# A macaron transformer block on one core: attention's eight half images begin at other slots, the last one has nine slots

## What is computed

```python
x = x + 0.5 * ffn(layernorm(x))
x = x + attention(layernorm(x))
x = x + 0.5 * ffn(layernorm(x))
```

## The kernel before

| list | half 0 to 7 |
|---|---|
| D_SLOT | 29, 37, 46, 55, 64, 72, 81, 90 |
| B_SLOT | 37, 46, 55, 64, 72, 81, 90, 98 |
| NORM_SLOT | 39, 48, 57, 66, 74, 83, 92, 100 |
| out | 41, 50, 59, 68, 76, 85, 94, 101 |
| EXP_SLOT | 31/33, 39/42, 48/51, 59/60, 66/69, 76/78, 83/86, 92/95 |

## Time and profile before

### The profile page before, as it was taken

One profiled execution on the slowest core, in us unless ns is written; L12 is line 12 of the kernel. 1 busy time (PEld: TensorE's weight loads), 2 busy tenths in 40 slices (PEclk: granted clock), 3 DMA queues, 4 the chain that ended last, 5 costly groups with the idle time before them and its releaser, 6 DMA issues.

```text
span 1469.7 us, 22015 instructions
## 1 busy us (share of the span) xinstructions
PE 1419.1 (97%) x7642; PEld 679.7 (46%) x7642; DVE 944.8 (64%) x1295; ACT 552.4 (38%) x1153; POOL 501.0 (34%) x424
## 2 busy tenths in 40 slices
PE   4999999999999999899999999999999999999998
PEld 2444444444444544445454444444444444444443
DVE  5778853333348989898889889979925733333243
ACT  4566323333233433345435454345233213333211
POOL 2321132221244475252625434444322122221353
PEclk9999999999999999999999999999999999999999
DMA  8999659887493467075526552445338168888594
GB/s 305 305 350 320 267 146 209 200 182 192 172 277 125 156 196 220 30 244 135 153 72 186 150 166 73 121 160 140 112 101 257 59 188 213 192 190 185 187 321 165
DMA packets 233724, 272.63 MB, mean 186 GB/s; under 512 B 132242, under 2 KB 156818, under 8 KB 230162
## 3 DMA queue, kind: packets, MB, share of 16 engines
q1 hardware_dynamic: 198594, 166.34, 39.7%
q10 hardware_dynamic: 23664, 67.66, 14.5%
q0 software_dynamic: 11360, 37.23, 9.4%
HBM read 168.39 MB, written 72.88 MB: 164 GB/s over the span
## 4 chain that ended last, share of the span: by engine, by line
PE 63%; DVE 10%; issue 8%; DMA 4%; POOL 2%; ACT 2%; SPq 1%; POOLq 0%; ACTq 0%; DVEq 0%
PE bank L1484 25%; PE bank L1607 13%; PE bank L1498 12%; PE bank L1632 7%; DVE region L1147 3%; DMA rows<-sorted_y,slots 1%; PE side L1120 1%; PE side L1620 1%; DVE region L1153 1%; POOL rows L665 1%; DMA x2d<-rows 1%; DVE sgh L1854 1%; PE side L1253 1%; DMA region<-region 1%; POOL hs L1812 1%
## 5 line engine op out<-in xcount | busy, mean ns | idle before, releaser
L1484 PE MATMUL bank<-xT,wb 128*128 128x512 bf16 x2688 | 615.5, 381 | 22.6 <-DMA xT<-region 17.6
L1484 PEld LDWEIGHTS bank<-xT,wb 128*128 128x128 bf16 x2688 | 257.7, 98 | 323.9 <-issue 29.2
L1812 POOL TENSOR_TENSOR hs<-sgh,hs 128x512 bf16<-128x512 f32 x126 | 161.9, 1285 | 629.1 <-ACT hs L1704 628.2
L1498 PE MATMUL bank<-wb,hs 128*128 128x512 bf16 x1536 | 358.0, 380 | 0.2 <-POOL hs L1812 0.2
L1498 PEld LDWEIGHTS bank<-wb,hs 128*128 128x128 bf16 x1536 | 147.8, 98 | 173.9 <-issue 2.9
L1607 PE MATMUL bank<-wr,region 128*128 x912 | 221.7, 379 | 0.0
L1704 ACT ACTIVATE hs<-sgh 128x512 bf16<-128x512 f32 x128 | 81.3, 635 | 340.2 <-DVE sgh L1854 337.4
L1854 DVE TENSOR_TENSOR sgh<-bank,sgh 128x512 f32<-128x512 f32 x128 | 87.9, 687 | 155.8 <-PE bank L1484 154.6
L1147 DVE TENSOR_TENSOR region<-region 128x1024 f32<-128x1024 f32 x128 | 183.0, 1454 | 0.9
L1801 POOL DMA_INDIRECT region<-xnd,idxs x78 | 74.6, 957 | 221.8 <-DMA region<-region 213.5
L1153 DVE TENSOR_REDUCE region<-region 128x256 f32<-128x2048 f32 x64 | 146.3, 2286 | 2.2
(11 more groups left out here) (182 smaller groups left out, 1351.6 us busy)
## 6 DMA issues: line engine op xcount, KB each, us to landing
wb<-wsplit ACTq DMA_DIRECT2D x42, 1024.0 KB
wb<-wsplit ACTq DMA_DIRECT2D x42, 512.0 KB, 4.4
sorted_y<-region SPq DMA_DIRECT2D x78, 256.0 KB
wsplit<-wb SPq DMA_DIRECT2D x8, 1536.0 KB, 7.4
wr<-wall SPq DMA_DIRECT2D x6, 1536.0 KB, 9.7
rows<-x SPq DMA_DIRECT2D x32, 256.0 KB, 4.9
region<-xln SPq DMA_DIRECT2D x128, 64.0 KB, 3.7
xnd<-rows SPq DMA_DIRECT2D x30, 256.0 KB, 4.0
```

The lines of the kernel that those rows point to most:

```text
L1484: m = e.matmul(ps[:], wb[:, w % 2, wp, at:at + P], xt[:, xp, c, :], start=(i == 0), stop=(i == 3 * NDC - 1))
L1498: m = e.matmul(psD[tt][:], hs[:, s % 2, hp, tt * P:(tt + 1) * P], wb[:, w % 2, wp, at:at + D], start=(first and i == 0), stop=(last and i ...
L1812: e.tensor_tensor(hs[:, s % 2, 1, :], sgh[:, s % 2, :], hs[:, s % 2, 0, :], ALU.subtract).then_inc(S("h_lo").sem, 1)
```

## The change

Three lists of slots get other values; no instruction is added or taken away.

```diff
-        EV_LOAD[0], EV_LOAD[1], EV_LOAD[2], EV_LOAD[3], EV_LOAD[5], EV_LOAD[6], EV_LOAD[8] = (
-            UNIT - 2, EV_AT[1] - 4, EV_AT[2] - 2, EV_AT[3] - 3, EV_AT[5] - 3, EV_AT[6] - 2, EV_AT[8] - 1)
+        EV_LOAD[0], EV_LOAD[1], EV_LOAD[2], EV_LOAD[3], EV_LOAD[4], EV_LOAD[5], EV_LOAD[6], EV_LOAD[8] = (
+            UNIT - 2, EV_AT[1] - 4, EV_AT[2] - 2, EV_AT[3] - 3, EV_AT[4] - 4, EV_AT[5] - 3, EV_AT[6] - 2, EV_AT[8] - 1)
...
-        D_SLOT = [ROUTED_AT[0] + 6 + 35 * h // 4 for h in range(HALVES)]
+        D_SLOT = [ROUTED_AT[0] + 6 + 9 * h - h // 3 for h in range(HALVES)]
         LOAD_SLOT = [ROUTED_AT[0] + 1, ROUTED_AT[0] + 5] + [d - 4 for d in D_SLOT[2:]]
-        B_SLOT = D_SLOT[1:] + [D_SLOT[-1] + 8]
+        B_SLOT = D_SLOT[1:] + [D_SLOT[-1] + 9]
```

## The result

The changed kernel took 1468.91 us in the median of ten runs (1466.22 to 1472.14), the kernel before, run between them, 1474.50 us (1469.81 to 1478.97). The ratio is 0.9964, 95% interval [0.9953, 0.9974]: 5.6 us or 0.36% faster, where 9.5 us were forecast. The forecast of 1463.4 us is missed by 5.5, of which 1.6 is the kernel before itself: its median is 1474.5 over ten runs, where the forecast started from 1472.9 over three. The result lies inside the range, a little above the point that was called faster. Of all runs behind this text one, of the kernel before, took 3854 us and is left out as slow.

What follows compares the result with a forecast made beforehand. TensorE's waits in attention were taken as all that a new order could give back. Terms 4.1 + 0.2 + 1.8 + 0 + 3.9 - 0.5 gave 9.5 us, from 1472.9 to 1463.4, range 1458.5 to 1470.5.

Steps and rivals of the forecast that it cites:

- half 1: Slots 40 to 47 with the combines: 6.4 us over the pieces falls to 2.3, seven combines falling in; gain 4.1.
- half 3: Slots 55 to 63: counted among nine-slot halves costing 0.1 us together; no gain or loss named.
- half 5: Slots 72 to 80, cut to eight slots: 2.0 us stays 2.0 (ends 0.5 and 5.4); gain 0.
- the routing: Slot 112 on: second routing list stands behind an evacuation, charged 0.5 us (0 to 1.5); later row gather stays hidden.
- half 7: Slots 90 to 98, given a ninth slot: 5.4 us over the pieces falls to 1.5; gain 3.9.
- half 4: Slots 64 to 71, given a ninth slot: silu and turn waits go, 2.1 us falls to 0.3; gain 1.8.
- half 2: Slots 48 to 54, cut to eight slots: slot 49's stall shrinks, 2.0 us falls to 1.8; gain 0.2.
- The drain of the table load: ScalarE's exp ahead of turn or out pieces: skill page's drain estimated at some 5.5 us against the change; left out.
- B: Rival, given back: eight slots cost wherever they are; gain 3 instead of 9.5 us, 1470.0; chance 0.15.
- D: Rival: VectorE's total is the same and waits only move to other slots; 1472.9 us; chance 0.05.
- A: Rival: halves 2 and 5 fit without stalls, half 1 leaves no residue; five us more, 1458.5; chance 0.14.
- C: Rival: VectorE overflows in halves 2 and 5 once over about 4.2 us behind TensorE; 1477.4 us; chance 0.06.

Runs made afterwards that it cites:

- run of three edits: Kernel before with nine slots in the last half, each half's first two qkv pieces later and the second eight combines one slot earlier: ratio 0.9974.
- the order alone: Kernel before with only the new order of halves 0 to 6, the last half keeping eight slots: ratio 0.9988.
- second comparison: The kernel before and the changed kernel run once more, both unchanged: ratio 0.9955 [0.9939, 0.9971].
- last half of nine alone: Kernel before with only the last half's ninth slot added, run twice: ratios 0.994 and 0.996.

## Why the prediction was half right

From the forecast gain of 9.5 us to the 4.2 between the two profiled executions: 2.4 too little in half 1, 2.0 lost in half 3, to which the sum gave no term, 2.1 lost in half 5, whose term was 0, and 0.2 in the routing; 1.1 more than forecast in half 7 and 0.3 more in half 4. The time lies inside the range by the range's width and by the clock, which no term of the sum names: at equal clock the gain is 3.4 us. As far as the sum goes that is luck.

**What bounds the kernel** was read rightly: TensorE's waits in attention are all that there was to gain, and the change moved only them.

**Half 7, 3.9 us forecast, 5.0 measured.** The mechanism and place are as said: the wait for L1198 in slot 99 is gone. The residue was put at 1.5 us and is 0.48, since t_out was in time and took ScalarE's two copies with it. The run with this edit alone shows the same 0.48.

**Half 1, 4.1 forecast, 1.7 measured (2.8 in the second execution).** This is the first step that failed. The wait for L1198 did shrink from 2.87 to 0.41, as forecast (that a moved combine does this shows in the run of three edits as well, where it went from 2.9 to 1.3), and with it went the clock's 1.7 us, which the sum had in its 4.3 without knowing it; slots 40 and 41 moved to 41 and 42 with 1.05 and 0.19 us, as forecast. What was not seen: half 2's rows are loaded from xln a slot later, too. SyncE's issues and the transposes that want them, in the kernel before and after:

```profile
554.95 3.86 SPq L1083 DMA_DIRECT2D region<-xln  x8
...
562.59 0.63 PE L1103 MATMUL side<-ident,region 128*128 128x128 f32 x4 [0.17 <-DMA region<-xln]
```

```profile
566.29 3.92 SPq L1083 DMA_DIRECT2D region<-xln  x8
```

The rows were there 7.6 us after the first issue before, and 8.7 after (574.95 above). In the seven executions that were looked at in which SyncE's order has this load a slot later, TensorE waited 0.8 to 2.5 us for it, and 0.2 at most in the six that have it and the combines where they were. In the slot to which it moved, ScalarE's queue issues a weight load of 1024 KB beside it (at 567.45), in the one that it left one of 512 KB (at 556.10), and the weights' queue took 38.7% of the DMA engines' time instead of 26.2%. That this is the reason is argued from these rows and was not tested by itself. The other wait that is new, of 1.1 us, for VectorE's L1854 in slot 44, is its backlog: a combine stands in that slot behind the 3.04 us wait for rows of x.

**Half 3, not costed, 2.0 lost.** The second failed step. The prediction counted half 3 in "nine slots each: 0.1 together" and asked only about length. But the half ahead of it lost a slot, so its tiles stand two slots ahead instead of three: slot 58 waits 0.72 for a third part, slot 62 1.12 for L1112. This was in the profile of before: half 5 there, nine slots behind one of eight, cost 2.0 for the same two waits. The prediction even names slot 61 as a place where exp comes to stand just ahead of a turn, but gives it no price. The term that it put at nothing is 2.0 us.

**Half 5, 0 forecast, -2.1 measured.** The third. Its ends were given as 0.5 and 5.4, and the value was left at 2.0 because "exp and turn stay neighbours". The overlap of VectorE's heavier slots with that turn is what it had wrong. Eight slots with the tiles three ahead is what half 7 was in the kernel before, and that cost 5.4. VectorE, 3.5 us late in slot 78 before, is 5.0 late now, and the wait for L1112 goes from 1.1 to 2.60. The experiment that gave it back its ninth slot took its 4.2 to 0.1.

**Half 4 (1.8 forecast, 2.1 measured) and half 2 (0.2 and 0.2)** hold. The silu wait only moved, from slot 49 (1.81) to slot 50 (1.62), where the text said that it would be under 1 us; and no wait for L1112 came up in slot 53, where one was forecast. The sum is right and its parts are not.

**The routing: 0.5 forecast, 0.7 measured.** The list is late by 0.60 us at 1188.52, and the first block of the second routing waits for nothing. The indices were done at 1191.2 instead of 1193, and the transposes were issued at 1195.09, forecast 1197. TensorE and VectorE there (it answers the earlier trace rows):

```profile
1188.52 0.75 PE L749 MATMUL side<-rows 128*128 128x78 bf16 x16 [0.60 <-DVE rows L743]
1189.11 1.46 PE L1498 MATMUL bank<-wb,hs 128*128 128x512 bf16 x6
...
1205.94 2.75 PE L1607 MATMUL side<-wr,region 128*128 x12
```

```profile
1191.21 0.20 DVE L758 TENSOR_TENSOR idxs<-rows 128x39 int32<-128x39 f32 x1
```

**The drain of the table load.** The Trainium skill, ScalarE: Activation LUTs, "What ACT_TABLE_LOAD costs", would have made exp in front of a turn cost some 1.4 us more for each load, by an estimate from its drain of about 1380 ns. The seven ScalarE rows above show two loads of 1.28 us with the ACTIVATE at once behind each (888.81 + 1.28 = 890.09, next at 890.11; 891.24 + 1.28 = 892.52, next at 892.54). No drain, and the sum was right to leave it out. The table loads themselves do lie in the chain that makes slot 79 late.

**The rivals.** B ("given back") has the time, 1470.0 against 1468.9, but not the reason: eight slots do not cost wherever they are. Half 6 with eight slots costs nothing in two kernels, half 2 costs what it cost with nine. Nor is it D as a whole, since half 7's gain is real and stays; but for halves 1 to 6 D's reason is what happened: the waits moved to other slots, and their sum stayed (12.6 and 13.2 us in slots 40 to 89 with the order alone). A falls with halves 3 and 5. C's overflow did not come, but its condition did in one place: VectorE's product of up and silu began 5.0 us behind in slot 78, and the wait there was 2.6 us, nothing like the 14 of C. A product took 1.482 us on average instead of 1.454.

**How much of the result is the clock.** At equal clock the gain is 3.4 us, which the stalls confirm (18.2 to 14.7, means of two executions each). The medians differ by 5.6. The rest goes with the granted clock (in the second comparison, 0.9952 for the runs of before and 0.9970 for those of the changed kernel): the wait of slot 46 brought it down in both executions of the kernel before, and no wait of attention did in either of the changed one. That portion, 1.7 us, belongs to what the change gave, though a comparison at equal clock leaves it out.

## What to carry to other kernels

When steps of a static schedule move against each other, cost each part not by its length but by everything that it meets, and look in the old trace for the part that already meets it so: its price can be read there, and of the seven halves here that were priced so and whose length or neighbours differed, three came within about 0.1 us, two inside their forecast of 0 to 1, and two were 0.7 off. List the parts that do not move but whose neighbours do, and for each moved load look at what else the DMA queues carry in its new slot. And where a gain is under one per cent, put runs beside each other at the same granted clock, and then ask of the trace which falls of the clock the change itself has taken away or brought.

## What the runs showed of the hardware that was not expected

**Waits of TensorE take the clock with them, in equal portions.** In the fourteen traces (two of before, twelve of changed ones) the granted clock falls from 1.00 to 0.50, 2.4 to 1.2 GHz, for 3.4 us or twice that, and each portion costs 1.7 us. Between 20 and 1405 us every fall begins in a wait or within 2 us behind it. Counted over all fourteen: each of 20 waits of 2.8 to 4.9 us had one or two portions with it or behind it; of 46 waits of 2.0 to 2.7 us 13 had; of 28 waits of 1.5 to 2.0 us none. What decides between these is not shown. Two equal waits can differ in this (slot 98 of the kernel before: 2.26 us twice, once with a fall behind it; slot 79: 2.60 without, 2.61 with two portions).

**This goes with most of what differs from run to run.** The runs of one kernel lie at granted clocks of 0.993 to 1.000, and their times follow it by about 1.5 us for each 0.001. One portion, 3.4 us at half clock of 1470, is 0.0012. The last half of nine alone ran at 1462.15 us in the run at clock 1.000 and at 1470.31 in one at 0.996.

**A wait outside of the change weighs as much as the change.** In all fourteen executions TensorE waits ahead of attention for half 0's rows in slots 26 and 27, 2.6 to 4.9 us, and in thirteen the clock falls there: 3.10 us in the kernel before, 3.63 and two portions in the one after. That is 2.2 us of clock and wait, most of why the two profiled spans differ by 1.9 us and not by 4.2.
